# First mixer of a four-layer program: three merged soft maxima a chunk, additions by 32-row matmuls into four PSUM banks, another order of the projection

## The reference, cut to what matters

```python
q = l2norm(silu(short_conv(x @ Wq.T, cq)));  k = l2norm(silu(short_conv(x @ Wk.T, ck)))
v = silu(short_conv(x @ Wv.T, cv));          lr = softplus(x @ Wlr.T + BASE_LR)
mask = tril(ones((CHUNK, CHUNK)))            # CHUNK = 16, so 16 chunks; D_INNER = 4
def step(carry, xs):
    W_in, W_out = carry
    q_t, k_t, v_t, lr_t = xs
    k_h = softmax(einsum('blhd,bDhd->blhD', k_t, W_in)) * lr_t[..., 1:]
    q_h = softmax(einsum('blhd,bDhd->blhD', q_t, W_in))
    qk = einsum('bqhD,bkhD->bhqk', q_h, k_h) * mask
    o_t = einsum('bqhD,bDhd->bqhd', q_h, W_out) + einsum('bhqk,bkhd->bqhd', qk, v_t)
    W_out = W_out + einsum('bnhD,bnhd->bDhd', k_h, v_t)
    for _ in range(2):
        g_out = -attn(W_in, k_t, v_t)        # softmax over the 16 tokens of the chunk
        g_in = -attn(W_out, v_t, k_t)
        W_in = W_in - lr_in * g_in
        W_out = W_out - lr_out * g_out
    return (W_in, W_out), o_t
```

## Time and profile before

| | us |
|---|---|
| median of 3 runs | 1147.15 (1146.93 to 1149.79) |
| the profiled execution, its own time | 1152.76 |
| its span in the trace | 1151.0 |
| load_x, until all streams end | 0 to 21.9 |
| layer_norm | 21.9 to 41.3 |
| l0_project | 41.3 to 116.5 |
| l0_scan | 116.5 to 388.4 |
| all after it | 388.4 to 1151 |
| PE busy / DVE busy over the span | 794.0 / 795.6 |
| granted TensorE clock, mean | 0.818 of full |

### The profile page before, as it was taken

One profiled execution on the slowest core, in us unless ns is written; L12 is line 12 of the kernel. 1 busy time (PEld: TensorE's weight loads), 2 busy tenths in 40 slices (PEclk: granted clock), 3 DMA queues, 4 the chain that ended last, 5 costly groups with the idle time before them and its releaser, 6 DMA issues. The chain is left out here.

```text
span 1151.0 us, 18519 instructions
## 1 busy us (share of the span) xinstructions
PE 794.0 (69%) x6214; PEld 633.6 (55%) x6222; DVE 795.6 (69%) x2279; ACT 428.0 (37%) x893; POOL 329.7 (29%) x480
## 2 busy tenths in 40 slices
PE   0577565675676465578999887247799998467775
PEld 0255354564555354467777766126588887235544
DVE  2654677777777575647767763376788899689485
ACT  0453211212111202456666642231366665343331
POOL 3520323323323304453456505430111110011131
PEclk9968567767766776869999999768899999579996
DMA  2000000000000003003000024200000000100000
GB/s 45 0 1 1 1 1 1 1 1 1 1 1 1 9 1 64 1 5 97 9 7 5 15 53 143 66 12 1 20 21 21 21 21 10 47 1 0 1 19 19
DMA packets 38436, 21.39 MB, mean 19 GB/s; under 512 B 9377, under 2 KB 37617, under 8 KB 38369
## 3 DMA queue, kind: packets, MB, share of 16 engines
q1 hardware_dynamic: 37120, 17.98, 6.2%
q0 software_dynamic: 1248, 2.57, 0.7%
HBM read 15.40 MB, written 5.13 MB: 18 GB/s over the span
## 5 line engine op out<-in xcount | busy, mean ns | idle before, releaser
L1678 DVE TENSOR_REDUCE l1a_low_top<-l1a_score 128x2 f32<-128x512 f32 (+1 forms) x96 | 66.2, 690 | 62.2 <-PE l1a_score L1555 36.2
L1646 ACT ACTIVATE l1a_weights<-l1a_score,l1a_low_top 128x128 f32<-128x128 f32 (+1 forms) x256 | 89.7, 425 | 44.6 <-DVE l1a_low_top L1678 33.2
L2269 PEld LDWEIGHTS l2e_down<-l2e_wd,l2e_hidden 128*128 128x128 f32 x512 | 66.2, 191 | 11.7 <-DVE l2e_hidden L2385 7.1
L1552 PE MATMUL l1a_score<-l1a_k_rows,l1a_q_of 128*128 128x128 f32 (+1 forms) x256 | 56.1, 327 | 22.9 <-ACT l1a_weights L1646 11.8
L2367 DVE SCALAR_TENSOR_TENSOR l2e_mixed<-l2e_down,l2e_scaled,l2e_mixed 128x128 f32<-128x128 f32 x256 | 71.7, 343 | 0.1
L1510 POOL TENSOR_TENSOR l1a_q_of<-l1a_q_rows,l_quad_of 128x1024 fp32r<-128x1024 f32 x32 | 59.9, 1895 | 38.5 <-ACT l1a_q_rows L1635 38.5
L2269 PE MATMUL l2e_down<-l2e_wd,l2e_hidden 128*128 128x128 f32 x512 | 68.3, 276 | 3.5 <-DVE l2e_hidden L2385 3.5
L1701 DVE COPY l1a_weightsT<-l1a_flip 128x512 f32<-128x512 f32 x96 | 65.5, 682 | 1.6 <-PE l1a_flip L1590 1.3
L230 PE MATMUL l_norm_turned<-eye,xn 128*128 128x128 f32 x48 | 13.7, 451 | 73.7 <-DVE xn L204 73.7
L1590 PE MATMUL l1a_flip<-eye,l1a_weights 128*128 128x128 f32 x384 | 61.3, 285 | 1.3 <-issue 0.7
L1552 PEld LDWEIGHTS l1a_score<-l1a_k_rows,l1a_q_of 128*128 128x128 f32 x256 | 41.1, 214 | 37.9 <-ACT l1a_weights L1646 21.6
(11 more groups left out here) (538 smaller groups left out, 2307.8 us busy)
## 6 DMA issues: line engine op xcount, KB each, us to landing
l1e_w<-in_l_w SPq DMA_DIRECT2D x46, 128.0 KB
l2e_wgu<-in_l_wgu SPq DMA_DIRECT2D x16, 128.0 KB, 2.1
l_rows<-l1r_rows SPq DMA_DIRECT2D x1, 1483.5 KB, 11.6
l1r_rows<-l_rows SPq DMA_DIRECT2D x1, 1483.5 KB, 7.3
x_sb<-in_x SPq DMA_DIRECT2D x4, 256.0 KB, 3.6
l1e_mixed<-l_done SPq DMA_DIRECT2D x4, 256.0 KB, 3.6
l2e_wd<-in_l_wd SPq DMA_DIRECT2D x16, 64.0 KB, 1.8
out<-x_sb SPq DMA_DIRECT2D x8, 128.0 KB, 1.8
```

What stands on the lines that cost most here:

```text
L1552: nc.tensor.matmul(bank[:, n * width:(n + 1) * width], q_of[i][:, h, tile * P:(tile + 1) * P], k_rows[i][:, h // 4, 0:width], start=n == 0 ...
L1646: last = nc.scalar.activation(weights[s % 2][:, n * width:(n + 1) * width], score[s % 2][:, n * width:(n + 1) * width], ACT.Exp, bias=low_ ...
L1678: nc.vector.tensor_reduce(low_top[:, s % 2, 0:len(heads)], score[s % 2][:, :].rearrange("p (h k) -> p h k", k=key_tiles * P), AX.X, ALU.ma ...
L2269: last = nc.tensor.matmul(down[c % 2][:, j, :], hidden[c % 2][:, j * P:(j + 1) * P], wd[i][:, :], start=True, stop=True)
```

## The change

1. **Constants later.** `Fast.load` becomes `load_weights` (the large weight DMA, right behind the four of x) and `issue`, which SP runs in layer_norm's block: 16 DMAs of taps, then 32 of first weights, ln_g and ln_b. The six memsets and the drawings of `Fast.zero` leave layer_norm's block; POOL does them in l0_project, in the order norms, rates, clear K, rate_wide, clear V, clear Q, later and first weights.
2. **Projection reordered.** K is projected first (near), then the rates, Q (far); V is projected last (far), after K's norms are scattered. The norms of both use banks 0 and 1 of near, in two halves. V's tokens are turned last, into far.
3. **Merged soft maxima.** Three a chunk: own (k and q over states, 128 columns), out (mid of the chunk before and now of this one, 128 columns), in (old and new, 128 columns). The exponentials are written to PSUM by ACT, the reciprocals to PSUM by DVE, and one transpose of 128 partitions takes the place of four of 32.
4. **Additions by 32-row matmuls.** W_in and W_out lie in four PSUM banks, one for each 32 rows; add now has eight matmuls, 32 token rows against 128 columns, 32 columns streaming. give_out becomes give_results: 16 matmuls of 32x32 and one of 128x128, one chunk later; POOL sums three of its four terms before (give_less).
5. **Masks from PSUM.** w_old, w_new and w_here are masked by DVE straight from the four banks; only w_mid still goes over ACT and POOL.

```diff
-            fast.load(sp)
+            fast.load_weights(sp)
...
+    def load_weights(self, sp):
+        sp.wait_ge(self.zeroed, 1)
+        sp.dma_start(self.weights[:, :, H:2 * H], self.weights_dram).then_inc(self.weights_in, 16)
+
+    def issue(self, sp):
         for h in range(H):
             own = slice(h * HD, (h + 1) * HD)
             sp.dma_start(self.taps[own, :, :], self.taps_dram[h].rearrange("(j d) t -> d j t", d=HD)).then_inc(self.consts_in, 16)
+        for h in range(H):
+            own = slice(h * HD, (h + 1) * HD)
             for j, dram in enumerate(self.first_drams):
-                sp.dma_start(self.first[own, j, :], dram[h].rearrange("i d -> d i"), allow_slow_non_contiguous=True).then_inc(self.consts_in, 16)
+                sp.dma_start(self.first[own, j, :], dram[h].rearrange("i d -> d i"), allow_slow_non_contiguous=True).then_inc(self.firsts_in, 16)
...
@@ l0_project, POOL @@
+                fast.draw_norms(order)
+                pool.nop().then_inc(norms_drawn, 1)
+                fast.draw_rates(order)
+                pool.nop().then_inc(rates_drawn, 1)
+                fast.clear_halves(K, 1)
                 pool.wait_ge(rates_ready, 1)
...
+                fast.clear_halves(V, 2)
+                fast.clear_halves(Q, 3)
+                fast.draw_scan(order)
                 pool.wait_ge(v_kept, SETS)
                 nc.gpsimd.tensor_tensor(fast.v_own[:, :, :, :], fast.v_toks[:, :, :, 0:OWN], fast.v_toks[:, :, :, OWN:P], ALU.add)
...
@@ l0_scan, PE @@
-                def add(out, toks, c, terms):
+                def add(out, toks, c, weights):
                     for g in range(2):
-                        last = nc.tensor.matmul(out[:, g * P:(g + 1) * P], toks[:, c, g, :],
-                                                terms[:, g, :, :].rearrange("p b s -> p (b s)"), start=False, stop=g == 1,
-                                                skip_group_check=True)
+                        for b4 in range(4):
+                            rows = slice(32 * b4, 32 * b4 + 32)
+                            last = nc.tensor.matmul(out[:, b4, g * STATE:(g + 1) * STATE], toks[rows, c, g, :], weights[rows, g, :],
+                                                    start=False, stop=False, skip_group_check=True)
                     return last
...
@@ l0_scan, DVE: the loop @@
+                    lower("own", c, DI)
+                    lower("out", c, CK, sets)
+                    if c >= 2:
+                        dve.wait_ge(less_ready, c - 1)
+                    weigh("own", c, DI, fast.token_rate[:, c, :, :], own[c % 2][:, :, :, :].rearrange("p s h i -> p (s h i)")).then_inc(ready["own"], 1)
+                    out = terms["out"][:, sets, :].rearrange("p s a -> p (s a)")
+                    order.then(weigh("out", c, CK, by_chunk[:, RATE_OUT, c - 1 + sets.start:c - 1 + sets.stop, :], out, sets))
+                    nc.vector.transpose(by_tokens["out"][:, sets, :, :].rearrange("p s g i -> p (s g i)"), out).then_inc(ready["out"], 1)
...
+                    dve.wait_ge(old_summed, c + 1)
+                    mask(w_old[c % 2], w_out_ps).then_inc(old_ready, 1)
...
+                        mask(w_new[c % 2], w_out_ps).then_inc(new_ready, 1)
+                        lower("in", c, CK)
+                        out = terms["in"][:, :, :].rearrange("p s a -> p (s a)")
+                        order.then(weigh("in", c, CK, rep(by_chunk[:, RATE_IN, c, :], 1, 2), out))
+                        nc.vector.transpose(by_tokens["in"][:, :, :, :].rearrange("p s g i -> p (s g i)"), out).then_inc(ready["in"], 1)
                         dve.wait_ge(in_summed, c + 1)
-                        mask(w_here[(c + 1) % 2], win_ps).then_inc(in_ready, 1)
+                        mask(w_here[(c + 1) % 2], w_in_ps).then_inc(here_ready, 1)
```

More of the change, by code:

```diff
@@ new lines, in pair @@
+        def pair(n, shape):
+            return [sb(f"{n}{i}", shape) for i in range(2)]
+        SETS = ("own", "out", "in")
+        w_old, w_new, w_mid, w_here = (pair(f"w_{n}", [P, 2, 4, STATE]) for n in ("old", "new", "mid", "here"))
+        mid_raw = sb("mid_raw", [P, 4, SET])
+        top, total, share = ({n: sb(f"{x}_{n}", [P, 2 * H]) for n in SETS} for x in ("top", "total", "share"))
+        shifted = {n: sb(f"shifted_{n}", [P, 2 * SET]) for n in SETS}
+        terms = {n: sb(f"terms_{n}", [P, 2, SET]) for n in SETS[1:]}
@@ new lines, in keep_result @@
+                def keep_result(c):
+                    act.wait_ge(result_made, c + 1)
+                    nc.scalar.copy(fast.out[:, c, :, :, :].rearrange("p g h d -> p (g h d)"), result_ps).then_inc(result_kept, 1)
+                for c in range(NCK):
+                    exponent("own", c)
+                    sets = sets_of(c)
+                    exponent("out", c, slice(sets.start * SET, sets.stop * SET), SCALE)
+                    act.wait_ge(turned_made, c + 1)
+                    nc.scalar.copy(turned[c % 2][:, :, :].rearrange("p g f -> p (g f)"), turned_ps).then_inc(turned_kept, 1)
+                    if c < LAST:
+                        exponent("in", c, scale=SCALE)
+                    if c:
+                        keep_result(c - 1)
@@ L820, in _, with lower @@
                 order = Order(dve, dve_order)
-                def lower(n, c):
+                def lower(n, c, size, part=slice(0, 2)):
                     dve.wait_ge(scored[n], c + 1)
-                    scores = score_ps[n][:, 0:2 * STATE].rearrange("p (a l) -> p a l", l=CK)
-                    order.then(nc.vector.tensor_reduce(top[n][:, :], scores, AX.X, ALU.max))
-                    nc.vector.tensor_tensor(shifted[n][:, :, :], scores, rep(top[n][:, :], 2, CK), ALU.subtract).then_inc(down[n], 1)
```

572 lines of the change are left out of this document (246 added, 326 removed).

## The result

The changed kernel takes 1088.8 us (median of 4 runs, 1086.1 to 1093.1) against 1147.5 (1146.9 to 1149.8) for the kernel before on the same chip: a ratio of 0.949, 95% interval 0.947 to 0.951. I had forecast 1099 us, 1070 to 1136. The profiled execution has a span of 1091.4 us against 1151.0, so 59.6 us went; my sum was -48.3. The two profiled executions lie 4.3 and 5.3 us above their medians, so the profiles may be compared.

What follows compares the result with a forecast made beforehand. No engine is full; a scan chunk is one chain hopping between engines, mostly on DVE, and side work ends the first stages. -16.2 + 5.3 - 37.4 (scan) = -48.3 on 1152.76, less 5.6 to the median: 1099 us, range 1070 to 1136.

Steps and rivals of the forecast that it cites:

- Constants later: Load and layer_norm: load ends at 7.2 us, SP's 50 DMAs end layer_norm at 25.1 instead of 41.3; -16.2 us.
- Projection: l0_project in its new order on PE takes 80.5 us (78 to 85) against 75.2; +5.3 us.
- The addition: Scan: sixteen 32-row instructions cost as much as the full additions, 1.22 us at low clock, 0.71 at full.
- A: The forecast itself: row tiles work side by side, mostly at low clock; 1080 to 1118 us, chance 0.62.
- D: Rival: an addition's 16 loads run one after another, chunk 20.2 us, 1183 us in all; chance 0.12.
- The chunk: Scan: one chunk takes 14.6 us instead of 17.0, from a chain of 15.1 at low clock and 12.2 at full.
- Rival B: PE's spread additions keep the clock at full in the scan: chunk 12.7 us, 1070 us in all; chance 0.10.
- That PE is late for the in set: Scan: PE is busy with give_results and grow until 12.0 us, while the in set's weighing ends at 11.35.
- The port: Scan: DVE's product with two SBUF inputs took 1.08 us beside POOL; reading one from PSUM saves 0.9 us.
- The mask from PSUM: Scan: DVE's mask of w_old straight from PSUM stands in the chunk's chain at 0.45 us.
- Start and last chunk: Scan beside 15 full chunks: start 3.9 us, first chunk 1.4 less than a full one, last about 13.
- E: Rival: merging does not shorten the scan's chain, as PE's output work fills it; about 1143 us, chance 0.03.

Runs made afterwards that it cites:

- e7: Changed kernel with 34 of the 50 small DMAs issued beside the projection and POOL's v_own sum moved into the scan; ratio 0.936 to the kernel before.
- e3: Changed kernel with six extra PE transposes a chunk, placed in gaps where PE waits; ratio 0.948 to the kernel before.
- e11: Changed kernel with the mask of w_old done by ACT's copy and POOL's product, as before the change; ratio 0.945 to the kernel before.
- e2: Changed kernel with every matmul of an addition reading rows 0 to 31, so one row group of the array; 1277.4 us in one run.
- e1: Changed kernel with a chunk's growth matmul issued in the next chunk, behind the scores of the out set; ratio 0.950 to the kernel before.
- e4: Changed kernel with the reciprocals written to SBUF instead of PSUM; ratio 0.960 to the kernel before.
- e10: Changed kernel with e7's two edits and twenty-eight extra PE transposes a chunk; 1032.1 us, ratio 0.909 to the kernel before.

## Why the prediction was right, step by step

**Constants later** (forecast -16.2, measured -15.8). SP sets the end of both stages, as said. That its list had no business beside the normalising is not in my sum: e7 took it out, 7.3 us. I read the normalising's 15.0 us before as its own length; it was 10.5 once POOL's clears were gone, a gain hidden behind SP in the changed kernel.

**Projection** (forecast +5.3, measured +4.3). The order of arrivals came out: K's convolution at 11.1 (10.9), K done at 45.4 (42 to 46), Q at 72.0 (70.5), v_own last, at 79.2, and the stage ends at 79.5 (78 to 85). The 1.0 us by which I missed is less than what the same code varies by (77.5 us in e3 and e11). Only the size of a few steps was off, the sum of Q's squares for one: 3.62 us where I had 4.9.

**The addition** (taken 1.22 at half clock and 0.71 at full; measured 1.08 and 0.65). The case that decided between A and D was right, for the reason given, and e2 shows it.

**The chunk** (forecast 14.6; measured 13.74). This is the term that was mis-sized: 0.86 us x 15 = 12.9 us, where the whole sum missed by 11.3 (the projection gave another 1.0; the scan's start and end took back 1.1, what follows the scan 1.1, and the constants 0.4). By the chain, from w_here's end (190.77): own ready at 2.9 (I had 3.3), out ready 4.2 (4.7), w_old 5.8 (6.4), w_new 7.4 (8.2), in ready 10.8 (11.35), PE free 11.4 (12.0), w_here 13.7 (15.1). Up to PE's release 0.6 us comes from additions of 1.08 for 1.22 and somewhat shorter steps; the other 0.8 lies behind it. That is 1.4 us less than the 15.1 of my chain, of which I had allowed for 0.5 by taking 14.6, a choice and not a sum. Behind PE's release I had both in additions at half clock, on the ground that the new chunk has shorter dense stretches. It has fewer, but the one stretch that is left (196.65 to 202.2, PE without a break) ends just where the chain needs PE. Rival B was thus true in part: the clock rises in each chunk, for 3.4 us of it (201.8 to 205.2), and e1 shows what that is worth in the ten chunks that lose it.

**That PE is late for the in set** was right (0.64 us). Taking the growth matmul out of the way gained nothing over the scan: 0.47 us a chunk was lost where the clock stayed down, 0.8 to 0.9 was won where it rose elsewhere (e1).

**The port**: 0.9 us a chunk in my chain; 0.54 in the instruction by e4, and 0.72 in the chunk with the clock that went with it. Right in kind; the instruction itself is worth three fifths of what I gave it.

**The mask from PSUM**: I put it in the chain at 0.45; it is there, at 0.42. But what it replaced would have cost the same (e11), which my sum, made of the new chain alone, never asked.

**Start and last chunk**: beside fifteen full chunks the scan had 234.5 - 219 = 15.5 us in my sum; it is 222.7 - 15 x 13.74 = 16.6.

**Two slips in the rivals.** A chunk at full clock was to take 12.2 us, with five additions at 0.71; but own's addition lies beside the chain, so four count, and my own terms give 15.1 - 4 x 0.51 - 0.65 = 12.4. Measured where the clock is full throughout: 11.75 (e10), so B's 12.7 was too long a chunk for what it describes. And E, no gain in the scan, was put at 1143 us, though the front's -10.9 would still have come: 1136.
